# Causal attention with a routed feed-forward on one core: the score products in array tiles of 64 by 64

## What is computed

```python
q = x @ wq_lat @ wq_heads          # k and v likewise, x layer-normalised before
att = einsum('bhqd,bhkd->bhqk', q, k) * SCALE
att = where(causal, att, -inf); att = softmax(att)
y = einsum('bhqk,bhkd->bhqd', att, v)
x = x + layernorm(y @ w_proj + b_proj)
ys = geglu(xf @ Ws1 + bs1) @ Ws2 + bs2          # shared feed-forward
w = softmax(top_k(logits, 2))                   # two of 12 experts a row
x = x + layernorm(ys + sum_e w_e * (geglu(xf @ We1[e] + be1[e]) @ We2[e] + be2[e]))
```

## Time and profile before

| | us |
|---|---|
| median of 3 runs | 1138.73 |
| lowest, highest | 1134.33, 1139.64 |
| the profiled execution | 1140.07 |
| its span, first to last instruction | 1138.3 |
| TensorE busy, matrix products | 1003.8 (88%) |
| VectorE, ScalarE, GpSimd busy | 824.6, 747.5, 632.6 |

### The profile page before, as it was taken

The page is one execution under the profiler, slowest core; times in us unless marked ns, Lnnn a source line. Parts: engine busy times, 40 slices in busy tenths (PEclk is TensorE's granted clock), DMA queues, the critical chain, the costliest instruction groups (busy, mean ns, idle before and its releaser), DMA issues. The chain is left out here.

```text
span 1138.3 us, 31487 instructions
## 1 busy us (share of the span) xinstructions
PE 1003.8 (88%) x8446; PEld 616.1 (54%) x8446; DVE 824.6 (72%) x2411; ACT 747.5 (66%) x1311; POOL 632.6 (56%) x1195
## 2 busy tenths in 40 slices
PE   4589999999999999978879998659999999999875
PEld 3453434434343444333456664338888888888632
DVE  5688888888888888867688995325666666665637
ACT  4578788888888888856546664316666666666626
POOL 4337777777777777754217777742444444444344
PEclk9899999999999999989968998869999999999988
DMA  8313333333333333342341111132222222221176
GB/s 221 102 30 110 106 111 110 106 108 112 110 105 108 105 106 112 112 125 73 102 160 52 56 54 55 50 82 54 62 64 66 58 67 59 64 62 51 41 240 206
DMA packets 135606, 107.47 MB, mean 94 GB/s; under 512 B 32203, under 2 KB 127874, under 8 KB 135538
## 3 DMA queue, kind: packets, MB, share of 16 engines
q1 hardware_dynamic: 124722, 87.45, 27.2%
q0 software_dynamic: 8544, 17.78, 4.3%
q10 hardware_dynamic: 2272, 1.45, 0.5%
HBM read 55.96 MB, written 50.69 MB: 94 GB/s over the span
## 5 line engine op out<-in xcount | busy, mean ns | idle before, releaser
L1670 DVE TENSOR_REDUCE maxima<-ps 128x8 f32<-128x1024 f32 x320 | 380.1, 1222 | 78.6 <-PE ps L1230 71.2
L945 ACT ACTIVATE pT_area<-ps 128x1024 f32<-128x1024 f32 x320 | 321.1, 1023 | 87.6 <-PE ps L1262 82.2
L840 POOL DMA_INDIRECT ys_dram<-quad_area,place_cur x139 | 133.1, 957 | 193.4 <-issue 138.2
L718 POOL TENSOR_SCALAR_AFFINE_SELECT pT_area<-pT_area 128x256 f32<-128x256 f32 (+1 forms) x448 | 186.5, 439 | 93.6 <-ACT pT_area L945 91.2
L1309 PE MATMUL ps<-pT_area,quad_area 128*32 128x512 f32 (+3 forms) x2048 | 187.5, 450 | 0.6 <-POOL pT_area L718 0.6
L830 POOL DMA_INDIRECT xs_dram<-quad_area,idx_cur x128 | 123.0, 961 | 76.7 <-issue 74.3
L1262 PE MATMUL ps<-quad_area 64*128 64x256 bf16 (+3 forms) x1024 | 127.1, 304 | 29.6 <-DMA quad_area<-mT_sb 27.5
L1529 PE MATMUL ps<-quad_area 128*128 128x256 f32 (+1 forms) x456 | 129.9, 367 | 7.2 <-issue 3.8
L1230 PE MATMUL ps<-quad_area 61*128 61x128 bf16 (+2 forms) x1792 | 127.4, 241 | 4.7 <-ACT pT_area L945 2.7
L1530 PE MATMUL ps<-quad_area 128*128 128x256 f32 (+1 forms) x456 | 128.4, 363 | 0.0
L1089 ACT ACTIVATE xnT<-ps,be_cur 128x256 f32<-128x256 f32 (+1 forms) x228 | 94.7, 447 | 47.4 <-PE ps L1530 47.0
(11 more groups left out here) (237 smaller groups left out, 1528.9 us busy)
## 6 DMA issues: line engine op xcount, KB each, us to landing
qk_dram<-split_area SPq DMA_DIRECT2D x192, 128.0 KB, 2.3
quad_area<-qk_dram SPq DMA_DIRECT2D x256, 96.0 KB, 2.2
row_area<-xs_dram SPq DMA_DIRECT2D x63, 132.0 KB
pT_area<-ys_dram SPq DMA_DIRECT2D x16, 512.0 KB, 5.2
pT_area<-in_L_ffn_We SPq DMA_DIRECT2D x12, 384.0 KB, 7.6
out_dram<-pT_area SPq DMA_DIRECT2D x7, 512.0 KB, 2.9
xs_dram<-row_area SPq DMA_DIRECT2D x5, 528.0 KB, 4.0
split_area<-in_L_ffn_We SPq DMA_DIRECT2D x12, 192.0 KB, 3.6
```

What stands on the lines that cost most here:

```text
L718: return pool.affine_select(out=blocks, in_=blocks, compare_op=ALU.is_ge, fill=0.0, base=0, pattern=[[0, count], [1, P]], channel_multipli ...
L840: pool.indirect_dma_start(ys_dram, at, ys[:, ns % 2, h, :], None).then_inc(s_yst[ns % 2], 16)
L945: act.activation(pT[:, gs % 2, n, :], ps[:, bank:bank + 2, :].rearrange("p a b -> p (a b)"), ACT.Exp).then_inc(s_exp, 1)
L1670: dve.tensor_reduce(to, ps[:, bank:bank + 2, :].rearrange("p a (j k) -> p a j k", k=P), AX, ALU.max).then_inc(s_mxf, 1)
```

## The change

All score products, of both kinds, are cut into tiles of 64 rows by 64 columns of the array: `later` 0 makes the first 64 queries (or keys) of a tile of 128 on partitions 0 to 63, `later` 1 the other 64 on partitions 64 to 127. So one quad has 100 products for its scores where it had 52.

In a diagonal unit the first 64 queries of a block no longer compute the block's upper 64 keys, which are all masked for them. They take the 64 keys ahead of the block and the block's first 64 keys instead, so that the part to be masked is the triangle in the upper half of the bank's columns for both halves of the queries. All those keys are permitted, and only the maximum is taken. Query tile 0 has no keys ahead: there key 0 is repeated 64 times. One mask product for each half and bank is then added onto the scores, after them, where there were two for each bank of 128 rows ahead of them. `mask_to` and `mask_of` shrink, and of the 14 selects that built them four remain.

All ring waits are set apart from the products, as well as the wait for the maxima's DMA.

```diff
-        mask_to = sb("mask_to", [P, 2, P], BF16)
-        mask_of = sb("mask_of", [P, 2, ROWS], BF16)
+        mask_to = sb("mask_to", [P, ROWS], BF16)
+        mask_of = sb("mask_of", [P, 1, ROWS], BF16)
...
-                for half in range(2):
-                    same = to[:, half, ROWS * half:ROWS * half + ROWS]
-                    chain(pool.affine_select(out=same, in_=same, compare_op=ALU.not_equal, fill=1.0, base=0,
...
-                for late, value in ((to[:, 1, ROWS:], 0.0), (to[:, 1, 0:ROWS], 1.0), (of[:, 1], MASKED)):
-                    chain(pool.affine_select(out=late, in_=late, compare_op=ALU.not_equal, fill=value, base=1 - ROWS,
-                                             pattern=[[0, ROWS]], channel_multiplier=1))
+                chain(pool.affine_select(out=to, in_=to, compare_op=ALU.not_equal, fill=1.0, base=0,
+                                         pattern=[[-1, ROWS]], channel_multiplier=1))
+                chain(pool.affine_select(out=of[:, 0], in_=of[:, 0], compare_op=ALU.is_ge, fill=MASKED, base=0,
+                                         pattern=[[-1, ROWS]], channel_multiplier=1))
...
-                if masks:
-                    wait_apart(pe, ready, done, s_passed)
-                else:
-                    pe.wait_ge(ready, done)
+                wait_apart(pe, ready, done, s_passed)
...
+                def half(rg, later, head, qt, at, keys, first, last=False):
+                    lo = qt * P + ROWS * later
+                    return pe.matmul(ps[ROWS * later:ROWS * later + ROWS, bank + rg, at:at + keys.shape[-1]],
+                                     rows(2 * rg + head, 0, lo, lo + ROWS, slot, ROWS - 3), keys, start=first, stop=last)
...
+                    for j, qt in enumerate(DIAGONALS):
+                        for rg in range(2):
+                            if qt == 0:
+                                half(rg, 0, u, qt, j * P + ROWS, key_rows(rg, u, 0, ROWS), True)
+                            else:
+                                half(rg, 0, u, qt, j * P, key_rows(rg, u, qt * P - ROWS, qt * P + ROWS), False)
+                        for rg in range(2):
+                            half(rg, 1, u, qt, j * P, key_rows(rg, u, qt * P, qt * P + P), qt == 0)
+                        if qt == 0:
+                            for rg in range(2):
+                                half(rg, 0, u, qt, j * P, key_rows(rg, u, 0, 1).broadcast_to([ROWS - 3, ROWS]), False)
+                    for later in range(2):
                         for rg in range(2):
                             row = slice(ROWS * rg, ROWS * rg + ROWS)
...
+                            late_keys = ps[ROWS * later:ROWS * later + ROWS, bank + rg, :].rearrange("p (j k) -> p j k", k=P)[:, :, ROWS:]
+                            last = pe.matmul(late_keys, mask_to[row], mask_of[row].broadcast_to([ROWS, NT, ROWS]), start=False, stop=True)
...
                 if nth(EXP_ORDER, gs, n) == 0:
-                    pe.wait_ge(s_m[slot], 8 * (g - slot) + 32)
+                    wait_apart(pe, s_m[slot], 8 * (g - slot) + 32, s_passed)
...
+                    for later in range(2):
+                        lo = kb * P + ROWS * later
+                        for rg in range(2):
+                            last = pe.matmul(ps[ROWS * later:ROWS * later + ROWS, bank + rg, at:at + w],
+                                             rows(2 * rg + head, 1, lo, lo + ROWS, slot, ROWS),
+                                             rows(2 * rg + head, 0, kb * P, T, slot, ROWS), start=True, stop=True)
```

More of the change, by code:

```diff
@@ L1206, in wait_emptied @@
                 quad = g - back + AHEAD[kind]
-                masks = items(gs)[at][0] == "max" and items(gs)[at][1] < 2
                 if kind == "max":
@@ new lines, in key_rows @@
+                def key_rows(rg, head, first, last):
+                    return rows(2 * rg + head, 1, first, last, slot, ROWS - 3)
+                if u < 2:
+                    for j, qt in enumerate(DIAGONALS):
[10 more added lines that the diff above has]
+                    for later in range(2):
@@ L1235, in scores_by_query @@
                         for rg in range(2):
                             row = slice(ROWS * rg, ROWS * rg + ROWS)
-                            keys = ps[:, bank + rg, :].rearrange("p (j k) -> p j k", k=P)[:, :, ROWS * half:ROWS * half + ROWS]
-                            of = mask_of[row, half:half + 1].broadcast_to([ROWS, NT, ROWS])
-                            pe.matmul(keys, mask_to[row, half], of, start=(half == 0), stop=False)
-                    for j, qt in enumerate(DIAGONALS):
-                        for rg in range(2):
-                            last = score(rg, u, j * P, qt, P, qt * P, j == NT - 1)
+                            late_keys = ps[ROWS * later:ROWS * later + ROWS, bank + rg, :].rearrange("p (j k) -> p j k", k=P)[:, :, ROWS:]
@@ L1243, in scores_by_query @@
+                            last = pe.matmul(late_keys, mask_to[row], mask_of[row].broadcast_to([ROWS, NT, ROWS]), start=False, stop=True)
                 elif u < 4:
                     for at, qt, keys in ((0, 1, P), (P, 3, 3 * P)):
-                        for rg in range(2):
-                            last = score(rg, u - 2, at, qt, keys, 0, None)
+                        for later in range(2):
+                            for rg in range(2):
+                                last = half(rg, later, u - 2, qt, at, key_rows(rg, u - 2, 0, keys), True, True)
@@ L1247, in scores_by_query @@
                 else:
                     for head in range(2):
-                        for rg in range(2):
-                            last = score(rg, head, 2 * P * head, 2, 2 * P, 0, None)
+                        for later in range(2):
+                            for rg in range(2):
+                                last = half(rg, later, head, 2, 2 * P * head, key_rows(rg, head, 0, 2 * P), True, True)
                 last.then_inc(s_mx, 1)
@@ L1260, in scores_by_key @@
                     w = T - kb * P
-                    for rg in range(2):
-                        last = pe.matmul(ps[:, bank + rg, at:at + w], rows(2 * rg + head, 1, kb * P, kb * P + P, slot, ROWS),
-                                         rows(2 * rg + head, 0, kb * P, T, slot, ROWS), start=True, stop=True)
+                    for later in range(2):
+                        lo = kb * P + ROWS * later
+                        for rg in range(2):
+                            last = pe.matmul(ps[ROWS * later:ROWS * later + ROWS, bank + rg, at:at + w],
+                                             rows(2 * rg + head, 1, lo, lo + ROWS, slot, ROWS),
+                                             rows(2 * rg + head, 0, kb * P, T, slot, ROWS), start=True, stop=True)
                 last.then_inc(s_st, 1)
```

7 lines of the change are left out of this document (removed).

## The result

The changed kernel takes 1164.51 us (median; 1161.23 to 1169.03), the kernel before 1138.99 us in the same comparison: ratio 1.0223, 95% interval 1.0193 to 1.0253. It is slower, by some 25 us, where 1137.7 us and a range of 1130 to 1147 us were predicted. The profiled execution took 1161.23 us, the lowest of its times, with a span of 1159.5 us; against the 1138.3 us of before that is +21.2 us. The traces explain these 21.2 us; what makes other executions longer by up to 8 us more is not in them.

What follows compares the result with a forecast made beforehand. It took each turn as one chain, SyncE's queue ending the first half and TensorE, VectorE and ScalarE the second, plus a start bound by GpSimd's masks. Start -3.0 and loop +2.0 gave -1.0 us: 1137.7 us median, range 1130 to 1147.

Steps and rivals of the forecast that it cites:

- The start, -3.0 us: Ahead of the first score at 47.60: ten of 14 mask selects go, the first root starts earlier, gaining 3.0 us.
- Four tiles together, 0.33 us for a diagonal unit: Diagonal units on TensorE: four tiles run side by side, so four mask products take 0.11 us instead of 0.22.
- Gain of the masks less loads, -0.32 + 0.10 us a half: Second half of a loop turn: mask products of three diagonal units gain 0.32 us, slower weight loads cost 0.10 us.
- Waits apart, price: TensorE's queue: a wait set apart costs 0.10 us where its release comes last, nothing where it came 0.15 us before.
- Their number: Second half of a turn: ring waits cost 0.17 us, two further places in a quad's first max unit 0.20 us.
- The first half hidden under SyncE's 0.18 us: First half of a turn: TensorE's added 0.15 us stays under the 0.18 us by which SyncE's queue is later, costing nothing.
- slower by waits: Rival, chance 0.18: waits or issue lengthen a half by 0.45 us; beyond 0.18 us the first half pays too, 1146.6 us.
- the loop's code stays resident: Loop code: forecast to stay loaded; the rival, chance 0.03, had 12 turns load it anew, 16 us, 1153 us.

## Why the prediction was wrong, point by point

- *The start, -3.0 us:* right in place and size. The first score came 2.92 us earlier, and the run with the masks built later keeps 3.1 us of it to the loop's end and is 0.36% shorter.
- *Four tiles together, 0.33 us for a diagonal unit:* right, 0.35 us. The weight loads of 64 columns were taken at 108 ns, and the page after has 108 and 106.
- *Gain of the masks less loads, -0.32 + 0.10 us a half:* wrong in its net size. With equal waits the tiles change a turn by -0.03 to +0.03 us. Which units give back what the diagonal ones gain was not followed.
- *Waits apart, price:* right each, 0.10 us. *Their number* was wrong. I counted two waits in a row a half, at the first units by query, and wrote that the wait for the maxima "already stands alone where it matters". It stood alone because the ring's wait rode on the load behind it. With that wait apart, the first units by key have two in a row as well: four places a half, 0.39 us instead of 0.20. With 0.09 us for the others a half grows by 0.47 us; measured (30.48 - 29.56) / 2 = 0.46 us.
- *The first half hidden under SyncE's 0.18 us:* the step that failed with it. The rival "slower by waits" had the right point of decision, 0.18 us, and came near the price beyond it (0.72 us a turn forecast, 0.92 measured), in part by luck: it took 0.25 us for each of two double waits a half, where four of 0.10 us were measured. I gave it 0.18.
- *The written-out steps:* never priced. I asked only if the loop's code stays resident, which it does, and left out that a packet must also arrive in time in steps that run once. It cost +9.6 us. With the waits back on the loads 7.2 us of it go, with before's units and waits all of it; waits apart with before's tiles don't stall. So the stalls take both, waits apart and 64 by 64 tiles. That late packets are the link is argued from where the stalls stand, each 1.27 to 1.56 us after a packet's end, and not shown. The Trainium skill, Runtime: NRT & Kernel Launch, Instruction fetch mechanics, says that crossing a 16 KiB block of code is mostly hidden; here it is so in the kernel before, while the changed kernel stands still for 1.89 and 1.60 us.

By these terms: -2.9 + 1.3 at the start, +9.6 in the written-out steps, 13 turns at 0.92 us = +12.0, and +1.3 behind them: +21.3, where the spans differ by 21.2 us. Most of these terms are stages of the same two traces, so the sum had to come out; what the separate runs confirm are the waits' price in the loop, the start's gain and what waits and tiles do in the written-out steps. Why waits apart should hold packets back stays open; no run here shows it.

## What to carry to other kernels

Count the waits that stand in a row on an engine's queue, not only those that come last: each costs its time of issue even when nothing is left to wait for, and here putting two on one instruction gave back 0.77 of the 0.95 us that all of them cost a turn. When a change adds instructions, look at the code's packets in the steps that run once, not only at the loop. And look for the part of a change that is worth having by itself: here it was the place of 14 selects, which needed none of the new tiles.

## What the runs showed of the hardware that I had not expected

- Two waits one behind the other on TensorE's queue are 0.15 us apart; with each such pair on one instruction a turn took 29.74 us instead of 30.51.
- Between products in tiles of 64 and of 128 columns there is a gap of about 0.1 us that products of equal width don't have (0.46 us for a diagonal unit instead of 0.35).
- From 65 to 105 us the packets of code of four kernels with waits apart started 3.7 to 6.3 us behind the grid, with the waits on the loads at most 2.9 us. TensorE stood still for up to 3.12 us inside a unit and went on 1.27 to 1.56 us after the packet's end.
- After stalls of 1.89 and 1.60 us the granted clock was 0.51, 1.2 GHz, for 6.5 and 3.4 us; after an idle time of 1.35 us in another kernel it stayed at 1.00.
